# Adding a residual to an open PSUM sum by an accumulating transpose instead of an identity matmul

## The chip, the core and the metric

The kernel runs on one core of a Trainium2 chip. The metric is the device time in microseconds (us). The engines are TensorE (PE; its weight loads are shown as PEld), VectorE (DVE), ScalarE (ACT), GpSimd (POOL) and SyncE (SP).

## The reference

The program chains four small attention layers over 32 sequences of 128 tokens with 128 features. The change touches only the first layer, which has 16 heads of 64 and three layer norms, each over a sum of a projection and a residual:

```
residual = input
sa = _mha(input, input, input, ..., causal=True)
x = _layer_norm(sa + residual, ln1_g, ln1_b)
residual = x
ca = _mha(x, encoder_output, encoder_output, ...)
x = _layer_norm(ca + residual, ln2_g, ln2_b)
residual = x
h = relu(x @ ffn_w1 + ffn_b1)
x = _layer_norm(h @ ffn_w2 + ffn_b2 + residual, ln3_g, ln3_b)
```

Layer 1 is another softmax attention (16 heads of 8), layer 2 consists of three linear-attention blocks with norms, and layer 3 is a softmax attention (8 heads of 16) followed by a recurrence over the 128 tokens.

## The kernel before

The 32 sequences are worked in 8 groups of G = 4 sequences, so a group has 512 token columns. Everything is float32 except the masks. Two streams share the engines: the *main* stream computes the first layer of group g, while the *side* stream computes layers 1 to 3 (up to the recurrence's inputs) of group g-1. `interleave` weaves the steps of the two streams by a fixed table of paces into one written-out order for each engine. So there are 8 main passes, 7 of them with a side stream beside them; then one side pass runs alone, and then come the recurrence (lines 935 and 939) and the output.

Each engine runs its own list strictly in order and waits on semaphores. For PSUM, main uses banks 0 to 4 and side uses banks 5 to 7. A bank is filled by PE (`filled`) and freed by the DVE or ACT instruction that reads it (`emptied`).

A layer norm of the main stream goes like this. POOL keeps `main_residual`, the residual plus the projection's bias, with the features on the partitions and 512 token columns (line 553). PE's item `(tag, "y")`, written by `sums` (lines 648 to 655), fills bank 0 with tokens on the partitions: for each of the 4 sequences it writes a 128x128 block as one accumulation group. For ln1 and ln2 the group is 8 matmuls of `headsT` with `w_o` and one matmul of `main_residual` with the identity. For ln3 it is 4 matmuls of `hidden` (the first four chunks of `headsT`) with `w_f2` and the same identity matmul. As `main_residual` is the stationary operand and the identity the moving one, the identity matmul adds its transpose, token by token. DVE then takes the moments (`bn_stats`, line 1145), POOL raises to the power -1/2, DVE normalises (line 1158), and PE transposes the result back (`turn4`, line 642).

`nc.tensor.transpose` is used elsewhere in the kernel for float32 blocks of the same size: for the probabilities (line 700), for the normalised rows and for `tok` (line 642). In all of these each write starts its own group. The names in the trace read moving operand, stationary operand: `ps<-ident,probs` is a transpose of `probs`, `ps<-ident,main_residual` the identity matmul of this change, and `ps<-w_o_ca,headsT` a projection.

Of the kernel before, what the change touches and what calls it, by code (L numbers as in the profile page):

```python
# [35 lines left out]
C0 = H0 * D0 // 128  # L36
# [3 lines left out]
FC0 = 4  # L40
# [79 lines left out]
def main_fills():  # L120

    order, n = [], 0
    for item in (x for step in MAIN_STEPS for x in step if x[1] not in NO_FILL):
        tag, kind = item[:2]
        if kind == "s":
            bank = item[2] % 2
        elif kind == "o":
            bank = 3
        elif kind == "y":
            bank = 0  # L130
        elif item[:3] == ("ca", "v", 1) and item[3] < 2:
            bank = (1, 3)[item[3]]
        else:
            bank, n = (2, 4)[n % 2], n + 1
        if kind in ("v", "y", "n"):
            by = "D"
        elif kind in ("k", "o") or tag in ("ffn", "in"):
            by = "AD"[item[-1] % 2]
        else:
            by = "A"  # L140
        order.append((item, bank, by))
    return order


def side_fills():

    order = []

    def attention(tag):
        per = SMALL[tag][0]  # L150
        for u in range(per * G + 2):
            if u >= 2 and (u - 1) % per == 0:
                order.append(((tag, "o", (u - 2) // per), 7, "D"))
            if 1 <= u <= per * G:
                order.append(((tag, "t", u - 1), 6, "AD"[u % 2]))
            if u < per * G:
                order.append(((tag, "s", u), 5, "A"))

    order += [(("l1", "q"), 5, "D"), (("l1", "k"), 6, "A"), (("l1", "v"), 7, "D")]
    attention("l1")  # L160
    for blk in ("en", "d0", "d1"):
        order += [((blk, "q"), 5, "D"), ((blk, "k"), 6, "D"), ((blk, "v"), 7, "A"),
                  ((blk, "kv", 0), 5, "D"), ((blk, "kv", 1), 6, "D"),
                  ((blk, "o", 0), 7, "D"), ((blk, "o", 1), 5, "D"), ((blk, "ot"), 6, "A"),
                  ((blk, "y"), 7, "D"), ((blk, "n"), 5, "D")]
        if blk != "d0":
            order += [((blk, "f", 0), 6, "A"), ((blk, "f", 1), 7, "A"),
                      ((blk + "f", "y"), 5, "D"), ((blk + "f", "n"), 6, "D")]
    order += [(("b3", "y"), 5, "D"), (("x3", "y"), 7, "D"), (("b3", "n"), 6, "D"), (("x3", "n"), 5, "D"),
              (("l3", "q"), 6, "D"), (("l3", "k"), 7, "A"), (("l3", "v"), 5, "A")]  # L170
    attention("l3")
    order += [(("l3", "ot"), 5, "A"), (("l3", "x"), 6, "D"), (("z3", "y"), 7, "D"), (("z3", "n"), 5, "D"),
              (("l3", "z"), 6, "A"), (("l3", "u"), 7, "D")]
    return order


MAIN, SIDE = Stream(main_fills()), Stream(side_fills())
# [69 lines left out]
def build_program(nc, I, out):  # L247
    with ExitStack() as ctx:
        def sb(name, shape, dt=F32):
            return ctx.enter_context(nc.sbuf_tensor(name, shape, dt))  # L250
# [7 lines left out]
        ident = sb("ident", [128, 128])  # L258
# [10 lines left out]
        w_o = {t: sb(f"w_o_{t}", [128, C0, E]) for t in ("sa", "ca")}  # L269
        bv_all = {t: sb(f"bv_all_{t}", [128, H0 * D0]) for t in ("sa", "ca")}  # L270
        w_f1 = sb("w_f1", [128, FC0 * 128])
        w_f2 = sb("w_f2", [128, FC0, E])
# [19 lines left out]
        main_residual = sb("main_residual", [128, GT])  # L292
# [3 lines left out]
        headsT = sb("headsT", [128, C0, GT])  # L296
        hidden = headsT[:, 0:FC0, :]
# [40 lines left out]
        residual = neg_q  # L338
# [56 lines left out]
        def bank(st, name):  # L395
            return ps[:, st.bank[name], :]
# [236 lines left out]
        def _(pe):  # L633
            mm = nc.tensor.matmul
# [4 lines left out]
            def turn4(st, name, src):  # L639

                for b in range(G):
                    last = nc.tensor.transpose(bank(st, name)[:, b * 128:b * 128 + 128], src(b), ident[:, :])  # L642
                last.then_inc(filled[st], 1)

            def one(st, name, lhs, rhs):
                mm(bank(st, name)[0:lhs.shape[-1], :], lhs, rhs, start=True, stop=True).then_inc(filled[st], 1)  # L646

            def sums(st, tag, terms):

                for b in range(G):  # L650
                    dst = bank(st, (tag, "y"))[:, b * 128:b * 128 + 128]
                    todo = list(terms(b))
                    for n, (l, r) in enumerate(todo):
                        last = mm(dst, l, r, start=(n == 0), stop=(n == len(todo) - 1))  # L654
                last.then_inc(filled[st], 1)

            def norm_turn(i, st, tag, slot):
# [3 lines left out]
            def token(x, b):  # L661
                return x[:, b * T:b * T + T]

            def before_filling(i, item, *needed):

                held = [MAIN.before[item]] if MAIN.before[item] is not None else []
                wait_all_emptied(pe, i, MAIN, held + list(needed))

            def project(i, item):
                tag, kind, n = item[:3]  # L670
                x = {"sa": xT["a"], "ca": xT["b"] if kind == "q" else cT}[tag]
                if item == ("ca", "v", 0, 0):
                    pe.wait_ge(loaded_ca, n_ca[0])

                needed = {("sa", "k", 0): [("in", 0), ("in", 1)], ("ca", "q", 0): [("ln1", "n")]}
                before_filling(i, item, *needed.get(item, []))
                if kind == "v":
                    one(MAIN, item, token(x, item[3]), w_qkv[tag][:, 2, n * 512:n * 512 + 512])
                else:
                    one(MAIN, item, w_qkv[tag][:, "qk".index(kind), n * 128:n * 128 + 128], x[:, :])  # L680
# [36 lines left out]
            def main(i):  # L717
                for step in MAIN_STEPS:
                    for item in step:
                        tag, kind = item[:2]  # L720
                        if tag == "in":

                            if kind == 0:
                                pe.wait_ge(group_in, i.at(48, 48))
                            turn4(MAIN, item, lambda b: (c_in if kind else x_in)[:, b, :])
                        elif tag == "ffn":
                            before_filling(i, item, ("ln2", "n"))
                            one(MAIN, item, w_f1[:, kind * 128:kind * 128 + 128], xT["a"][:, :])
                        elif kind in ("q", "k", "v"):
                            if item == ("sa", "v", 0, 0):  # L730

                                pe.wait_ge(masks_taken, i.at(1, 1))
                            project(i, item)
                        elif kind == "s":
                            scores(i, item)
                        elif kind == "t":
                            turn(i, item)
                        elif kind == "o":
                            outputs(i, item)
                        elif kind == "y":  # L740
                            pe.wait_ge(main_residual_ready, i.at(3, MAIN_LN.index(tag) + 1))
                            if tag == "ln3":
                                before_filling(i, item, *[("ffn", c) for c in range(FC0)])
                                sums(MAIN, tag, lambda b: [(token(hidden[:, c, :], b), w_f2[:, c, :]) for c in range(FC0)]
                                     + [(token(main_residual, b), ident[:, :])])
                            else:
                                t = "sa" if tag == "ln1" else "ca"
                                before_filling(i, item, *[(t, "o", u) for u in range(UNITS)])
                                sums(MAIN, tag, lambda b: [(token(headsT[:, c, :], b), w_o[t][:, c, :]) for c in range(C0)]
                                     + [(token(main_residual, b), ident[:, :])])  # L750
                        elif kind == "n":
                            before_filling(i, item, (tag, "y"))
                            turn4(MAIN, item, lambda b: main_normed[:, b, :])
                            if tag == "ln3":
                                wait_emptied(pe, i, MAIN, item)
                    yield
# [148 lines left out]
            def setup_side():  # L905
# [19 lines left out]
                yield  # L925

            passes(pe, main, side, setup_side())


# [20 lines left out]
            with pe.Fori(0, GROUPS // 2) as g:  # L950
                for n in range(2):
                    mm(ps[:, n, :], w_c[:, :], ub[:, bass.ds(g * 2 * G + n * G, G), :], start=True, stop=True).then_inc(fin_mm, 1)
                for n in range(2):
                    pe.wait_ge(fin_add, g * 2 + (n + 1))
                    for b in range(G):
                        last = nc.tensor.transpose(ps[:, 2 + n, b * 128:b * 128 + 128],
                                                   fin_sum[n][:, b * T:b * T + T], ident[:, :])
# [476 lines left out]
```

## Time and profile before

| | |
|---|---|
| median of 3 runs | 2710.94 us (2707.78 to 2711.83) |
| profiled execution | 2722.7 us, its span 2721.0 us |
| PE busy | 2321.0 us (85% of the span), 11161 instructions |
| DVE / ACT / POOL busy | 1502.9 / 1168.8 / 340.7 us |
| mean granted TensorE clock | 0.903 of full speed |

The profile page describes one profiled execution. A PE row counts machine instructions: a matmul of the program can be more than one of them, and every MATMUL has its LDWEIGHTS on the PEld row. The ends of matmuls are modelled and overlap with the next ones, so what a matmul costs is read from the distance of the starts and not from its duration. The profiled execution is 11.8 us longer than the median of the timed runs.

### The profile page before, as it was taken

The numbers are of one execution on the slowest core, as the hardware profiler recorded it, in microseconds if no ns is written. First come the engines' busy times: TensorE is split into PE (matmuls) and PEld (weight loads), VectorE is DVE, ScalarE is ACT, GpSimd is POOL, SyncE is SP. The second block draws the span as 40 slices with busy tenths as digits, with TensorE's granted clock in tenths as the row PEclk, the third lists the DMA queues.
The fourth block names the chain that finished last, engine by engine and source line by source line (L and its number), as shares of the span: only waits on it lengthen the run. The fifth ranks groups of instructions, "written<-read, shape, count | busy, mean of one in ns | idle before, by whom it ended". The sixth has DMA issues, their size and how long they took to land.

```text
span 2721.0 us, 32500 instructions
## 1 busy us (share of the span) xinstructions
PE 2321.0 (85%) x11161; PEld 1613.0 (59%) x11161; DVE 1502.9 (55%) x3998; ACT 1168.8 (43%) x4001; POOL 340.7 (13%) x349
## 2 busy tenths in 40 slices
PE   5887988898888988898889888998889888865898
PEld 3555655666565665565556656566556555543596
DVE  4554666565756666566656674666656665233212
ACT  3452635364544645363536454454536353210221
POOL 0002011101112011201110111101120121012000
PEclk9988999999999999999999998999999999566555
DMA  5000000000000000000000000000000000000001
GB/s 152 1 1 13 1 1 1 13 2 1 1 1 13 1 1 1 13 1 1 1 13 1 1 1 1 13 1 1 1 5 1 1 1 1 0 0 0 1 0 31
DMA packets 24511, 19.75 MB, mean 7 GB/s; under 512 B 1699, under 2 KB 22182, under 8 KB 24358
## 3 DMA queue, kind: packets, MB, share of 16 engines
q1 hardware_dynamic: 24358, 17.78, 2.3%
q8 instruction: 87, 1.43, 0.2%
q14 instruction: 66, 0.54, 0.1%
HBM read 15.68 MB, written 2.10 MB: 7 GB/s over the span
## 4 chain that ended last, share of the span: by engine, by line
PE 65%; DVE 21%; ACT 7%; issue 4%; POOL 3%; SPq 0%; DMA 0%; POOLq 0%; DVEq 0%
PE ps L646 13%; PE ps L654 8%; PE ps L787 7%; PE ps L689 7%; PE ps L712 6%; PE ps L770 4%; PE ps L780 4%; DVE tok L1158 3%; PE ps L700 3%; ACT probs L977 3%; DVE keys L1225 2%; PE ps L939 2%; PE ps L642 2%; DVE stats L1145 2%; POOL kx L563 2%
## 5 line engine op out<-in xcount | busy, mean ns | idle before, releaser
L977 ACT ACTIVATE probs<-ps,neg_max 128x128 f32<-128x128 f32 x1024 | 361.8, 366 | 419.4 <-DVE neg_max L1138 412.6
L977 ACT ACTIVATE s_probs<-ps,s_max 128x128 f32<-128x128 f32 x768 | 218.8, 367 | 274.0 <-DVE s_max L1138 273.9
L689 PE MATMUL ps<-keys,queries 128*128 128x256 f32 x1024 | 281.3, 398 | 28.4 <-ACT queries L971 28.4
L712 PE MATMUL ps<-probsT,values 128*128 128x256 f32 x1024 | 277.8, 395 | 3.7 <-ACT headsT L1011 2.7
L787 PE MATMUL ps<-kx,qT 32*128 32x512 f32 (+1 forms) x384 | 244.5, 720 | 33.5 <-POOL kx L563 33.5
L1138 DVE TENSOR_REDUCE neg_max<-ps 128x4 f32<-128x512 f32 x256 | 176.4, 689 | 162.7 <-PE ps L692 161.4
L1138 DVE TENSOR_REDUCE s_max<-ps 128x4 f32<-128x512 f32 x192 | 132.5, 690 | 235.7 <-PE ps L787 233.5
L689 PEld LDWEIGHTS ps<-keys,queries 128*128 128x128 f32 x1024 | 187.4, 195 | 119.6 <-ACT queries L971 42.4
L540 POOL TENSOR_TENSOR rstd<-var_eps,minus_half 128x4 f32<-128x4 f32 x88 | 90.3, 1026 | 1235.3 <-DVE var_eps L1151 1234.6
L1145 DVE BATCH_NORM_STATS2 stats<-ps 128x6 f32<-128x128 f32 x352 | 78.2, 284 | 299.4 <-PE ps L654 295.6
L712 PEld LDWEIGHTS ps<-probsT,values 128*128 128x128 f32 x1024 | 178.8, 194 | 67.3 <-issue 25.1
L977 ACT ACTIVATION_READ_ACCUMULATOR probs<-ps,neg_max 128x1 f32 x1024 | 208.7, 204 | 0.0
L700 PEld LDWEIGHTS ps<-ident,probs 128*128 128x128 f32 x1024 | 123.5, 142 | 128.2 <-issue 81.9
L971 ACT ACTIVATE probsT<-ps 128x512 f32<-128x512 f32 x256 | 155.7, 608 | 50.7 <-PE ps L700 49.5
L770 PEld LDWEIGHTS ps<-l1v,s_probsT 128*128 128x128 f32 x1024 | 143.9, 209 | 51.9 <-issue 49.3
L700 PE MATMUL ps<-ident,probs 128*128 128x128 f32 x1024 | 158.6, 278 | 0.4 <-DVE probs L1181 0.4
L642 PE MATMUL ps<-ident,tok 128*128 128x128 f32 x352 | 61.6, 302 | 103.8 <-DVE tok L1158 89.6
L646 PE MATMUL ps<-xT_a,w_qkv_sa 128*128 128x512 f32 x256 | 132.1, 603 | 12.8 <-DVE cT L1210 11.0
L780 PE MATMUL ps<-ident,s_probs 128*128 128x128 f32 x768 | 133.0, 300 | 10.3 <-ACT s_probs L977 7.3
L534 POOL TENSOR_TENSOR pool_scratch<-minus_half 128x1 f32<-128x1 f32 x88 | 17.0, 193 | 985.0 <-DVE x1T L1275 672.1
L770 PE MATMUL ps<-l1v,s_probsT 128*128 128x9 f32 x1024 | 137.1, 261 | 0.7 <-ACT s_probsT L971 0.7
L1240 DVE COPY headsT<-ps 64x256 f32<-64x256 f32 x256 | 107.5, 420 | 40.3 <-PE ps L712 38.2
(211 smaller groups left out, 4088.9 us busy)
## 6 DMA issues: line engine op xcount, KB each, us to landing
x_in<-in_x SPq DMA_DIRECT2D x8, 256.0 KB, 3.0
c_in<-in_ctx SPq DMA_DIRECT2D x8, 256.0 KB, 3.3
skip_in<-in_mask_BxS_ik SPq DMA_DIRECT2D x8, 256.0 KB, 3.1
out<-x_all SPq DMA_DIRECT2D x8, 256.0 KB, 2.3
valid_in<-in_mask_BxS_bf SPq DMA_DIRECT2D x8, 64.0 KB, 3.4
w_qkv_sa<-in_L_xattn_sa_wq SPq DMA_DIRECT2D x1, 512.0 KB
w_qkv_sa<-in_L_xattn_sa_wk SPq DMA_DIRECT2D x1, 512.0 KB
w_qkv_sa<-in_L_xattn_sa_wv SPq DMA_DIRECT2D x1, 512.0 KB
```

Source lines behind the costliest of these rows:

```text
L646: mm(bank(st, name)[0:lhs.shape[-1], :], lhs, rhs, start=True, stop=True).then_inc(filled[st], 1)
L654: last = mm(dst, l, r, start=(n == 0), stop=(n == len(todo) - 1))
L689: mm(bank(MAIN, item)[:, n * 256:n * 256 + 256], queries[:, c % 2, at], keys[:, c % 2, :, at], start=(n == 0), stop=False, skip_group_chec ...
L700: last = nc.tensor.transpose(bank(MAIN, item)[:, h * 128:h * 128 + 128], probs[:, u % 3, h * 128:h * 128 + 128], ident[:, :])
L712: last = mm(bank(MAIN, item)[:, n * 256:n * 256 + 256], values[:, c // 4, b0 + n, (c % 4) * 128:(c % 4) * 128 + 128], probsT[:, u % 2, n * ...
L770: last = mm(bank(SIDE, (tag, "o", b))[:, at:at + d1], s_probsT[:, u % 2, h * 128:h * 128 + 128], value[:, b, q * 4 + h, :], start=True, st ...
L780: last = nc.tensor.transpose(bank(SIDE, (tag, "t", u))[:, h * 128:h * 128 + 128], s_probs[:, u % 2, h * 128:h * 128 + 128], ident[:, :])
L787: mm(bank(SIDE, (tag, "s", s)), qT[part, b * T:b * T + T], kx[part, :, b * T:b * T + T], start=True, stop=True).then_inc(filled[SIDE], 1)
L971: A(dst, view(s) if view else s, fn, **kw).then_inc(emptied[st, "A"], 1)
L977: last = A(dst[:, u % dst.shape[1], h * 128:h * 128 + 128], bank(st, (tag, "s", u))[:, h * 128:h * 128 + 128], ACT.Exp, bias=src_max[:, u ...
L1138: V.tensor_reduce(dst[:, u % 2, :], bank(st, (tag, "s", u)).rearrange("p (h k) -> p h k", h=4), AX.X, ALU.max, negate=True).then_inc(max_r ...
L1145: last = V.bn_stats(stats[:, slot, b, :], bank(st, (tag, "y"))[:, b * 128:b * 128 + 128])
```

## The change

`sums` gets an argument `residual`. With it, the accumulation group is left open after the last projection matmul, and the group is closed by a matmul with `is_transpose=True` and `start=False` on the same operands as before. The three calls of the main stream's norms use it. The calls of the side stream pass no residual and are as they were. Nothing is reordered, no wait or semaphore is added or removed, and the program has the same list of instructions on each engine.

```
-            def sums(st, tag, terms):
+            def sums(st, tag, terms, residual=None):

                 for b in range(G):
                     dst = bank(st, (tag, "y"))[:, b * 128:b * 128 + 128]
                     todo = list(terms(b))
                     for n, (l, r) in enumerate(todo):
-                        last = mm(dst, l, r, start=(n == 0), stop=(n == len(todo) - 1))
+                        last = mm(dst, l, r, start=(n == 0), stop=(residual is None and n == len(todo) - 1))
+                    if residual is not None:
+                        last = mm(dst, token(residual, b), ident[:, :], start=False, stop=True, is_transpose=True)
                 last.then_inc(filled[st], 1)
...
-                                sums(MAIN, tag, lambda b: [(token(hidden[:, c, :], b), w_f2[:, c, :]) for c in range(FC0)]
-                                     + [(token(main_residual, b), ident[:, :])])
+                                sums(MAIN, tag, lambda b: [(token(hidden[:, c, :], b), w_f2[:, c, :]) for c in range(FC0)],
+                                     main_residual)
...
-                                sums(MAIN, tag, lambda b: [(token(headsT[:, c, :], b), w_o[t][:, c, :]) for c in range(C0)]
-                                     + [(token(main_residual, b), ident[:, :])])
+                                sums(MAIN, tag, lambda b: [(token(headsT[:, c, :], b), w_o[t][:, c, :]) for c in range(C0)],
+                                     main_residual)
```

## Rows read from the trace of the kernel before

**Rows 1.** The page: span, busy times, the slices of PE and its clock, the chain.

```profile
span 2721.0 us, 32500 instructions
PE 2321.0 (85%) x11161; PEld 1613.0 (59%) x11161; DVE 1502.9 (55%) x3998; ACT 1168.8 (43%) x4001; POOL 340.7 (13%) x349
...
PEclk9988999999999999999999998999999999566555
...
PE 65%; DVE 21%; ACT 7%; issue 4%; POOL 3%; SPq 0%; DMA 0%; POOLq 0%; DVEq 0%
```

**Rows 2.** Lines 654 and 700: count, duration ns min/median/max, first and last start.

```profile
L654 PEld LDWEIGHTS ps<-ident,main_residual x192: 192/192/212, 106.1 to 2299.3; 128*128 128x128 f32 x192
L654 PE MATMUL ps<-ident,main_residual x192: 275/275/276, 106.2 to 2299.4; 128*128 128x128 f32 x192
...
L700 PE MATMUL ps<-ident,probs x1024: 272/273/421, 40.4 to 2270.5; 128*128 128x128 f32 x171
```

**Rows 3.** Timeline, 499.9 to 512.5 us: start, length, engine, line [idle before, releaser].

```profile
499.81 0.96 PE L770 MATMUL ps<-l3v,s_probsT 128*128 128x17 f32 x8
...
503.00 2.02 PE L654 MATMUL ps<-w_o_ca,headsT 128*128 128x128 f32 x16 [1.04 <-DVE headsT L1240]
...
505.08 1.95 PE L654 MATMUL ps<-w_o_ca,headsT 128*128 128x128 f32 x16
...
507.09 1.95 PE L654 MATMUL ps<-w_o_ca,headsT 128*128 128x128 f32 x16
...
510.89 0.39 PE L654 MATMUL ps<-ident,main_residual 128*128 128x128 f32 x2
...
511.11 0.60 PE L642 MATMUL ps<-ident,tok 128*128 128x128 f32 x4
511.31 0.89 DVE L1145 BATCH_NORM_STATS2 stats<-ps 128x6 f32<-128x128 f32 x4 [8.46 <-PE ps L654]
511.75 0.60 ACT L971 ACTIVATE kx<-ps 128x512 f32<-128x512 f32 x1 [10.98 <-PE ps L642]
```

**Rows 4.** Timeline of PE, 420 to 432 us: transposes, then a matmul.

```profile
425.41 0.60 PE L700 MATMUL ps<-ident,probs 128*128 128x128 f32 x4
425.85 1.03 PE L712 MATMUL ps<-probsT,values 128*128 128x256 f32 x4
```

**Rows 5.** The chain that ended last, in order of time: start, length, what.

```profile
104.35 8.28 PE ps L654 x72
...
228.51 4.72 PE ps L654 x40
...
369.46 8.29 PE ps L654 x72
...
1253.79 8.29 PE ps L654 x72
...
1546.37 8.29 PE ps L654 x72
...
1844.15 8.29 PE ps L654 x72
...
2274.69 8.28 PE ps L654 x72
...
2294.99 4.72 PE ps L654 x40
```

**Rows 6.** Three ln2 sums by windows: PE, PEld, DVE, ACT, POOL busy, granted clock, DMA.

```profile
205.79:215.61 9.82, 9.80 (x72) 9.62 (x72) 0.00 (x0) 0.00 (x0) 0.00 (x0) 0.84 0.01 2
...
503.00:511.28 8.28, 8.28 (x74) 8.28 (x75) 0.00 (x0) 0.00 (x0) 0.00 (x0) 1.00 0.01 2
1680.15:1690.04 9.89, 9.88 (x74) 9.89 (x75) 0.00 (x0) 0.00 (x0) 0.00 (x0) 0.83 0.00 0
```

**Rows 7.** Timeline of PE, 204 to 218 us: the head of the first of them.

```profile
205.79 3.55 PE L654 MATMUL ps<-w_o_ca,headsT 128*128 128x128 f32 x16 [1.49 <-DVE l_bo L1128]
```

**Rows 8.** Groups by line and shape: count, busy us, mean ns of one, idle before.

```profile
L770 PE MATMUL ps<-l3v,s_probsT 128*128 128x17 f32 x512 | 69.0, 268 | 0.7 <-ACT s_probsT L971 0.7
```

## The prediction

> **What bounds the kernel now.** I read the page first. PE is busy for 85% of the span and holds 65% of the chain that ended last; DVE has 21%, ACT 7% and POOL 3% [rows 1]. So time taken off PE counts wherever PE is what the others wait for. The question is whether it is in the sums that are changed.
>
> Second comes the chain in order of time [rows 5]. Each sum of a main norm is a piece of its own in it: a piece of 72 PE instructions for ln1 and ln2, a piece of 40 for ln3. I counted 16 pieces of the first kind (first at 104.35 us, last at 2274.69 us) and 8 of the second (first at 228.51, last at 2294.99): 2 and 1 for each of the 8 passes. All 24 sums are therefore on the chain, in their full length (8.28 and 4.72 us).
>
> Third is the timeline around one sum [rows 3]. The sum starts at 503.00 and the DVE instruction that reads it starts at 511.31, having been idle for 8.46 us, released by PE's line 654. ACT had been idle for 10.98 us when it got the transpose that PE does right behind the sum. During the sum DVE and ACT do nothing at all: their busy times in that window are zero, and POOL's too [rows 6]. So no other work stands beside a sum that could become the later one when the sum gets shorter, and PE's own list behind the sum moves up with it.
>
> **What is removed.** The program has 8 passes x 3 norms x 4 sequences = 96 identity matmuls of `main_residual`. The trace has 192 MATMUL and 192 LDWEIGHTS for them [rows 2]: a float32 matmul is two machine instructions of each kind. The duration (275 ns) is not the price, since they overlap. The price is the distance of starts: from 505.08 to 507.09, 2.01 us, PE starts 18 instructions (16 of the projection and 2 of the residual) [rows 3], which is 0.1117 us each. All 192 ran at this speed: their durations lie between 275 and 276 ns [rows 2]. Removed: 192 x 0.1117 = 21.4 us.
>
> **What is added.** 96 float32 transposes of 128x128. The same form stands in the trace at line 700: the 8 passes have 8 x 32 units of 4 transposes, 1024 in all, and the trace has 1024 MATMUL for them [rows 2]: one machine instruction each, not two. Four of them start at 425.41, and the next matmul at 425.85 [rows 4]: 0.44 / 4 = 0.110 us each. Added: 96 x 0.110 = 10.6 us.
>
> The sum is 10.6 - 21.4 = **-10.9 us** (before rounding), 0.113 us for each residual and 0.45 us for each of the 24 sums. A sum of 72 instructions becomes one of 68 and should last 7.83 in place of 8.28 us; one of 40 becomes 36, 4.27 in place of 4.72 us.
>
> **Changing over between the two kinds.** The changed group goes matmul, transpose, matmul, and the kernel before has both crossings. From matmul to transpose: the last two residual instructions start at 510.89 and the transposes of `tok` at 511.11 [rows 3], 0.22 us for two instructions, the usual distance. From transpose to matmul: the 0.110 us above holds the crossing from line 700 to line 712 already [rows 4]. So the crossing is worth nothing. What the trace does not show is a transpose that adds to a block that the matmul just ahead is still writing. I bound its slot. From below: matmuls that move only 17 columns start every (0.96 - 0.268) / 7 = 0.10 us [rows 3, 8], so a full 128x128 float32 load does not let two starts come closer. That would be 96 x 0.10 = 9.6, and -11.8 us. From above: the transpose runs without overlap for its whole 0.273 us [rows 2], 96 x 0.273 = 26.2, which is +4.8 us. I take 0.110, the row of the same operation. Plain matmuls add to the block of their predecessor at the full rate already in these very sums, and that is the reason to stay at this end.
>
> **What comes behind.** Nothing is reordered and no wait is new. `filled` is raised by the last transpose in place of the last matmul, and the modelled length of both is alike (273 against 275 ns) [rows 2]. DVE's moments, POOL's root and the rest come 0.45 us earlier after every sum. POOL's `main_residual` is made before the sum as it was, and PE's wait for it was never the last one (the trace names DVE for it [rows 3]).
>
> **The clock.** Two of the 16 long sums took 9.82 and 9.89 us, at a granted clock of 0.84 and 0.83, where the usual one takes 8.28 at 1.00 [rows 6]. The delay is in the head: the first 16 matmuls take 3.55 in place of 2.02 us [rows 3, 7], after PE had been idle for the DVE (1.49 us). These are two levels, 2.4 GHz and 1.2 GHz, mixed in one stretch. The clock also makes equal passes unequal: from ln1's sum to the next pass's it is 292.6 us (1253.79 to 1546.37) and then 297.8 us (1546.37 to 1844.15), with a mean of (1844.15 - 369.46) / 5 = 294.9 us [rows 5]. Passes that get 1.36 us shorter meet the clock's changes at other places, and the total can move by some microseconds either way from that alone. The three timed runs differ by 4 us, which is my measure of it.
>
> The Trainium skill (TensorE: Matmul & The Clock Gate, Part 4: PE-mode transpose) says that the full clock does not engage for transposes since they do not count as PE being busy in the same way. By that rule a sum with 4 transposes among 32 matmuls would keep the full clock less surely. The rows of this kernel speak against its mattering: the four transposes at 425.41 started every 0.11 us, the full rate. The same page's terms table calls the transpose mode 4 times faster for float32, which applied to the removed 0.223 us would be 0.056 us for a transpose and -16.1 us in all; the 0.110 us of line 700 doesn't agree.
>
> **The rivals.**
> - *The transpose is cheaper between matmuls.* At line 700 transposes follow each other with a load each, so 0.110 us could be the load's pace. If a lone one took half a slot, the gain is 96 x (0.2234 - 0.056) = 16.1 us: 2694.8. Against it: the load of 128x128 float32 is needed here too, and matmuls of 17 columns are no closer than 0.10 us. Chance 5%.
> - *Half is given back.* Something other than the sum would have to end the waits behind it, or the clock would take it back, say in the passes that are now well placed (292.6 us): 2705.5. For it: the spread of the passes. Against it: every sum is on the chain, with DVE and ACT idle. Chance 8%.
> - *The clock falls in more sums.* The price is 9.82 - 8.28 = 1.54 us for each, so 7 more of the 24 eat the gain, and 12 more give 18.5 - 10.9 = +7.6: 2718.5. Against it: only 4 of 36 starts are transposes. Chance 4%.
> - *The accumulating transpose drains the array (the slower side).* Place: the end of each of the 96 groups. If the transpose waits until the matmul ahead has written and the next group waits for the transpose, each costs 0.273 + (0.275 - 0.112) = 0.436 us, 41.9 us in all against 21.4 removed, +20.5: 2731. With the first wait alone it is +4.8: 2716. It decides from a slot of 0.223 us on. Against it: both crossings show nothing. Chance 4%.
> - *The change does not do what it says*, that is, the accumulating form still becomes two instructions with two loads: 0, 2711. Line 700's one instruction speaks against it. Chance 3%.
>
> **How the numbers follow.** The forecast has 76%. Against the profiled execution it is 2722.7 - 10.9 = 2711.8 us; that execution lies 11.8 us above the median of the runs, and no step of mine depends on why, so the timed result is 2710.94 - 10.9 = **2700.1**, given as 2700. The likeliest case's own range is 2695 to 2706 (the bounds -11.8 and the clock's few microseconds). The range for 8 in 10 takes in the cheaper transpose in part and the half given back: 2693 to 2708. A measurement of this kernel can tell about 0.2%, 5.4 us, from no change. Faster by more than that: nearly all of the forecast, half of the second rival and the first one, 79%. Within it: the rest of these, the change that does nothing and the drain with one wait, 14%. Slower: most of the clock rival and the full drain, 7%.
>
> **What would show it.** In the changed profile the residual's row has 96 MATMUL and not 192, PE has 11161 - 96 = 11065 instructions, up to missing records, the pieces of the chain read x68 at about 7.83 us and x36 at about 4.27 us, and DVE's idle time before the moments shrinks by 0.45 us each. I am wrong if a group's starts show a gap beside the transpose, if more sums run with a granted clock under 1.00, or if the sums are shorter and the passes are not.

## The result: slower by 0.3%, with the work saved as forecast

| | before | after |
|---|---|---|
| median | 2709.7 us (9 runs, 2707.78 to 2714.22) | 2718.54 us (9 runs, 2716.18 to 2722.37) |
| profiled execution | 2722.7 us, span 2721.0 | 2716.18 us, span 2714.4 |
| ratio after / before | | 1.0031 (95% interval 1.0023 to 1.0040) |

The forecast was 2700 us (2693 to 2708), so it was wrong in sign. Later the changed kernel ran again beside before in two other groups of runs (e5 and e12 below). It took 2718.92 and 2719.00 us there, with ratios of 1.0030 (1.0019 to 1.0041) and 1.0006 (0.9995 to 1.0017). So its own time repeats to 0.5 us, and what varies is before, whose median lay between 2709.7 and 2717.24 us from group to group. The 0.3% holds in two of the three comparisons; in the third no difference is shown. The page of the profile after, against [rows 1]:

```profile
span 2714.4 us, 32308 instructions
PE 2314.5 (85%) x11065; PEld 1598.9 (59%) x11065; DVE 1503.5 (55%) x3998; ACT 1168.9 (43%) x4001; POOL 340.3 (13%) x349
...
PEclk9998999899999999999989999999989999566555
...
PE 65%; DVE 21%; ACT 7%; issue 4%; POOL 3%; SPq 0%; DMA 0%; POOLq 0%; DVEq 0%
```

PE starts 11065 instructions, 96 fewer, as forecast. The residual's own rows, against [rows 2], from the view of line 656:

```profile
L656 PEld LDWEIGHTS ps<-ident,main_residual x96: 142/143/175, 106.9 to 2295.2; 128*128 128x128 f32 x96
L656 PE MATMUL ps<-ident,main_residual x96: 272/273/273, 107.0 to 2295.3; 128*128 128x128 f32 x96
```

One sum in the timeline after (start, length, engine, line), against [rows 3]:

```profile
798.20 1.95 PE L654 MATMUL ps<-w_o_ca,headsT 128*128 128x128 f32 x16
799.98 0.27 PE L656 MATMUL ps<-ident,main_residual 128*128 128x128 f32 x1
800.09 1.95 PE L654 MATMUL ps<-w_o_ca,headsT 128*128 128x128 f32 x16
...
803.77 0.27 PE L656 MATMUL ps<-ident,main_residual 128*128 128x128 f32 x1
...
804.09 0.89 DVE L1147 BATCH_NORM_STATS2 stats<-ps 128x6 f32<-128x128 f32 x4 [8.00 <-PE ps L656]
```

A sequence takes 800.09 - 798.20 = 1.89 us where it took 2.01, there is no gap on either side of the transpose, and DVE is idle for 8.00 us before the moments where it was 8.46. So the sum is 0.46 us shorter at full clock (forecast: 0.45). The local forecast holds; the total does not follow it.

### The profile page after: what moved, and what is told of

Read it like the earlier page. It is cut to its first block, busy times and chain, and to the rows that moved or that the text cites. A ratio compares the mean times of both kernels' runs of the same rounds, so it can differ in the third digit from the quotient of the medians.

```text
span 2714.4 us, 32308 instructions
## 1 busy us (share of the span) xinstructions
PE 2314.5 (85%) x11065; PEld 1598.9 (59%) x11065; DVE 1503.5 (55%) x3998; ACT 1168.9 (43%) x4001; POOL 340.3 (13%) x349
## 4 chain that ended last, share of the span: by engine, by line
PE 65%; DVE 21%; ACT 7%; issue 4%; POOL 3%; SPq 0%; DMA 0%; POOLq 0%; DVEq 0%
PE ps L646 14%; PE ps L654 8%; PE ps L789 7%; PE ps L691 7%; PE ps L714 6%; PE ps L772 4%; PE ps L782 4%; PE ps L702 3%; DVE tok L1160 3%; ACT probs L979 3%; DVE keys L1227 2%; PE ps L941 2%; PE ps L642 2%; DVE stats L1147 2%; POOL kx L563 2%
```

## Where the time went: the clock, pass by pass

The first profile of before was of an execution 11.8 us above the median of its three runs, and in span the changed kernel is even shorter than that one. For a comparison I need an execution of before that is like its timed runs. Run e1 (below) gave one: 2710.55 us, span 2708.8 us, the fastest of its twelve. Here are its passes, cut at the start of the transposes of `x_in`. The columns are: the stretch, its length, the busy times of PE, PEld, DVE, ACT and POOL, the granted clock, DMA.

```profile
18.20:237.30 219.10, 173.61 (x803) 117.25 (x803) 109.78 (x264) 98.18 (x356) 8.34 (x9) 0.95 0.12 34
237.30:532.30 295.00, 259.13 (x1317) 178.10 (x1317) 182.53 (x480) 142.86 (x484) 41.96 (x41) 0.97 0.01 4
532.30:829.40 297.10, 261.35 (x1316) 179.26 (x1316) 182.49 (x480) 142.86 (x484) 41.96 (x41) 0.96 0.01 4
829.40:1123.00 293.60, 257.29 (x1317) 177.28 (x1317) 182.87 (x480) 142.87 (x484) 42.19 (x41) 0.98 0.01 4
1123.00:1416.50 293.50, 257.23 (x1316) 177.17 (x1316) 182.79 (x480) 142.87 (x484) 42.20 (x41) 0.98 0.01 4
1416.50:1710.00 293.50, 257.26 (x1316) 177.24 (x1316) 182.80 (x479) 142.86 (x484) 42.19 (x41) 0.98 0.01 4
1710.00:2003.60 293.60, 257.26 (x1317) 177.24 (x1317) 182.84 (x480) 142.86 (x484) 42.19 (x41) 0.98 0.01 4
2003.60:2560.70 557.10, 445.80 (x1908) 293.97 (x1908) 262.88 (x712) 191.53 (x614) 75.95 (x73) 0.79 0.00 1
```

The same view of the changed kernel:

```profile
18.10:235.50 217.40, 171.96 (x792) 115.51 (x791) 109.82 (x265) 98.11 (x356) 8.33 (x9) 0.95 0.12 34
235.50:532.60 297.10, 261.24 (x1305) 178.90 (x1305) 182.49 (x480) 142.57 (x484) 41.91 (x41) 0.96 0.01 4
532.60:827.10 294.50, 257.79 (x1305) 176.14 (x1305) 182.90 (x480) 142.59 (x484) 42.13 (x41) 0.97 0.01 4
827.10:1120.80 293.70, 257.43 (x1305) 176.38 (x1305) 182.60 (x480) 142.58 (x484) 41.88 (x41) 0.97 0.01 4
1120.80:1415.80 295.00, 258.67 (x1305) 177.08 (x1305) 182.56 (x480) 142.58 (x484) 41.90 (x41) 0.96 0.01 4
1415.80:1711.40 295.60, 259.59 (x1304) 177.26 (x1304) 182.57 (x480) 142.58 (x484) 41.90 (x41) 0.96 0.01 4
1711.40:2006.30 294.90, 258.62 (x1304) 177.02 (x1304) 182.56 (x480) 142.56 (x484) 41.89 (x41) 0.96 0.01 4
2006.30:2566.30 560.00, 448.98 (x1896) 294.44 (x1897) 262.75 (x712) 191.16 (x614) 75.60 (x73) 0.78 0.00 1
```

I number the passes from 0, so the first row is pass 0 and the last row is pass 7 with the side pass behind it. In this execution, before settles from the fourth row on into passes of 293.5 us with a clock of 0.98, each like the last to 0.1 us. The changed kernel does not: its passes take 293.7 to 297.1 us at 0.96 to 0.97. DVE, ACT and POOL have the same busy times in all. The first pass is 1.7 us shorter after, the six with a full side stream are 4.5 us longer together where 6 x 1.36 = 8.2 us less was due, and the last row is 2.9 us longer.

The clock's share: the engine spends twice the missing clock at the low level (1.2 GHz), so e1 has 2 x (1 - 0.907) x 2708.8 = 504 us of it and the changed kernel 2 x (1 - 0.900) x 2714.4 = 543 us. These 39 us more cost 5.6 + 10.9 = 16.5 us, or 0.42 us each, if the forecast saving is all there. Before's own runs give this price without that assumption: e1's slowest run has 2 x (1 - 0.902) x 2724.7 = 534 us of low time and is 15.9 us longer than the fastest with 504 us, which is about 0.5 us for each us more. So the low time is enough to eat the saving, and there is no sign that the saving is missing.

A second look is where both kernels meet the same low stretches. Before's pass of 297.1 us has them at about -1 (double length), 122, 142, 224 (double) and 279 us after its start. So has the changed kernel's of 295.6 us, all within 1 us of these. The difference is 1.5 us; forecast for a pass were 1.36. Alone this would be weak: e10's passes of 296.9 us have the same five stretches too, and are only 0.2 us shorter than before's where 0.67 was due. The firmest sign of the saving stays the sum itself, 0.46 us shorter in the timeline above.

## The experiments

Theory A: only the shorter sums matter; they put the work elsewhere against the clock's changes, and the passes then meet more low stretches. Rival B: the transposes themselves keep the clock up less well. Four kernels at a time ran on one chip and shared the runs of before. The three groups had before at 2717.24 us (e1 to e4), 2711.54 (e5 to e8) and 2715.92 (e9 to e12).

**e1: before again.** No edit.

> The kernel before, unchanged, to get a second trace of it with the granted clock of every run. Theory A (the saving of 10.9 us on PE is real, and the changed kernel's clock is low for longer because its work lies elsewhere against the clock's changes): about 2710 us, ratio 1.000, with a mean clock above the 0.898 of the changed kernel's runs, by so much that the low time explains some 20 us. Rival B (transposes keep the clock up less well than matmuls): the same for this run.

2715.86 us, ratio 1.0001 (0.9987 to 1.0015). Its 12 runs go from 2710.55 us at a clock of 0.907 to 2726.46 us at 0.902, a wider spread than I had allowed for. The changed kernel's nine lie at 0.897 to 0.900: at a lower clock than any run of before for which the clock is on record, and still faster than before's slowest.

**e2: half of the residuals.** The start count of the changed kernel without a transpose.

```
                     todo = list(terms(b))
+                    if st is MAIN and b not in (0, 2):
+                        todo = todo[:-1]
```

> The kernel before without the identity matmul in sequences 1 and 3 of each group of 4, so the residual is left out for half of the sequences. It starts exactly as many PE instructions fewer as the changed kernel (4 in each of the 24 sums, 0.45 us), and has no transpose in a sum. Theory A (only the shorter sums and where they put the work against the clock): like the changed kernel, about 2718 us. Rival B (transposes count less for the clock): 2710 - 10.7 = 2699 us, the saving comes out in full.

2715.34 us, ratio 0.9993 (0.9982 to 1.0004), clock 0.898 to 0.900. Of the saving of 10.7 us about 2 us are left in the medians, with no transpose in a sum.

**e3: transposes with the old length.** The edit is to the changed kernel.

```
+                    if residual is not None:
+                        nc.tensor.transpose(dst, token(residual, b), ident[:, :])
                     for n, (l, r) in enumerate(todo):
```

> The changed kernel with one more transpose of main_residual ahead of each group (the group's first matmul overwrites it), so that each sum has the length of the kernel before, with 8 transposes in it. Theory A: the time of the kernel before, about 2710 us. Rival B: more transposes and so more low clock, at least the 2718 us of the changed kernel and up to 2718 + 20.

2728.67 us, ratio 1.0042 (1.0028 to 1.0056). My number for A missed and B's came in. The trace shows how: passes 1 and 2 are 294.7 and 297.1 us, as before's; then where before goes over to 293.5, this one stays at 296.9 to 297.0 us for the four that are left. The padded sum is not quite as long as before's: from its first start to the next item's it lasts 8.05 us (796.05 to 804.10) against 8.11 (503.00 to 511.11 [rows 3]), and the ln3 sum is shorter by as much, so a pass has about 0.2 us less work. Whether that or the transposes hold it back, e3 can't tell. e9 does.

**e4: no residuals.** `b not in ()` in e2's edit.

> The kernel before with no identity matmul in any sum of the main stream, so the residual is left out. Each of the 24 sums is 0.89 us shorter, 21.4 us in all. Rival B: 2710 - 21.4 = 2688.6 us. Theory A: not in line with the saving; the 21.4 us less what the clock takes or gives, anywhere from 2680 to 2710 us, since the work lies elsewhere once more.

2706.7 us, ratio 0.9959 (0.9945 to 0.9972): 11 us faster where the work is 21.4 us less, clock 0.902 in the profiled run. Again some 10 us are lost, and there is no transpose in a sum.

**e5: after again.** No edit.

> The changed kernel, unchanged, on this chip beside the padded ones. Theory A (each pass is 1.36 us shorter at equal clock, and what decides the total is how often the passes meet the clock's low stretches): its passes alternate between about 294.9 and 295.6 us again, so 2716 to 2719 us and the same against the kernel before within 0.4%. Rival B (transposes in a sum lower the clock): clearly slower than the kernel with half of the residuals left out, which has the same count of instructions.

2718.92 us, ratio 1.0030 (1.0019 to 1.0041). The passes alternate between 295.6 and 294.9 us from the third to the sixth, as expected.

**e6: padded plus one.** e3 with this in front of the transposes of `x_in`, k = 1:

```
+                            if kind == 0:
+                                for _ in range(k):
+                                    nc.tensor.transpose(bank(MAIN, item)[:, 0:128], x_in[:, 0, :], ident[:, :])
                             turn4(MAIN, item, lambda b: (c_in if kind else x_in)[:, b, :])
```

> The padded kernel (e3), with one more transpose at the start of each of the 8 main passes, overwritten by the next: 8 x 0.11 = 0.9 us more work. Theory A: the passes of e3 stay at 297.0 us with 7 low pieces each because each begins just short of the place from which the kernel before goes over to 293.5 us; 0.11 us more carries pass 3 or 4 past it, and the kernel gets faster by up to 5 x 3.5 = 17 us, about 2712 us, although it does more. Rival B: slower than e3 by 1 us, about 2729 us.

2727.58 us, ratio 1.0059 (1.0045 to 1.0073): a miss for A as I had put it. The passes did not leave the long pattern; they took 296.9 to 297.0 us as in e3. But the run could not test A. The added transpose falls into a wait: the next matmuls on PE's list read `x_side`, and PE waits there for VectorE. In e3 they start at 1125.40, 1.12 us after the pass (1124.28), and in e6 at 1132.23, 1.13 us after it (1131.10). So nothing behind the transpose came later, and the equal passes say nothing about the clock. The same holds for e7, where the rows stand.

**e7: before plus one.** The same edit on before, k = 1.

> The kernel before with one more transpose at the start of each main pass: 0.9 us more work. Theory A: passes of 293.6 us from the third on, and since they begin 0.1 us later against the clock's grid each time rather than 0.02 us earlier, they do not fall back as some runs of the kernel before do: 2709 to 2713 us, not slower than before and less scattered. Rival B, or any theory by work alone: 0.9 us slower than before, about 2718 us.

2720.87 us, ratio 1.0040 (1.0026 to 1.0053), from 5 runs. Here is the start of pass 5, first in e1 and then in e7 (start, length, engine, line, idle time before):

```profile
1416.50 0.66 PE L642 MATMUL ps<-ident,x_in 128*128 128x128 f32 x4 [1.55 <-DVE xT_b L1171]
1417.63 1.16 PE L646 MATMUL ps<-x_side,turned 128*128 128x512 f32 x2 [0.47 <-DVE qT L1258]
...
1417.11 0.33 PE L727 MATMUL ps<-ident,x_in 128*128 128x128 f32 x1 [1.55 <-DVE xT_b L1174]
...
1418.24 1.13 PE L646 MATMUL ps<-x_side,turned 128*128 128x512 f32 x2 [0.36 <-DVE qT L1261]
```

The matmuls of `x_side` start 1.13 us after the pass in both; PE's wait for VectorE is 0.11 us shorter and takes in the added transpose. The profiled execution (span 2712.6 us, the fastest of the five) has the passes that A named: 297.1 us in pass 2, then 293.6, 293.5, 293.6, 293.5. As the added work is hidden, that is no support for A. The timed runs missed A's 2709 to 2713 us: four of the five have a clock of 0.902 or 0.903, where 12 of the 17 runs of before in the same group have 0.907 or 0.908. So an instruction that fits into a wait of PE went with a kernel 9 us slower in the median, at a lower clock.

**e8: after plus three.** The same edit on after, k = 3.

> The changed kernel with three more transposes at the start of each main pass: 0.33 us each pass, 2.6 us of work in all. By work alone: 2.6 us slower than e5. Theory A: the alternation of 294.9 and 295.6 us cannot hold, the passes take another pattern, and the time differs from e5 by something other than 2.6 us, of either sign and up to 10 us.

Three transposes no longer fit into the wait: the matmuls of `x_side` start 1.55 us after the pass (823.98 to 825.53) and not 1.13. The time is 2715.47 us, ratio 1.0010 (0.9998 to 1.0022), against e5's 2718.92 and 1.0030 (1.0019 to 1.0041): 3.4 us less, with 2.6 us more work. The intervals touch, so that it is faster is likely and not certain; that it is 2.6 us slower is excluded. Passes 3 and 4 are 295.6 and 294.9 us as in e5; the last two (1414.50 to 2003.60) are not: 292.9, then 296.2 us.

**e9: one residual less in a pass.**

```
+                    if tag == "ln3" and b == 3:
+                        todo = todo[:-1]
```

> The kernel before without one identity matmul in each pass (ln3, the last sequence of each group, whose residual is left out): 2 PE starts less in each pass, 0.22 us, 1.8 us in all, and no transpose in any sum. Theory A (pass length against the clock's grid): a pass that meets the long pattern is now about 0.2 us too short to leave it, as with the padded kernel, and stays at 297.0 us with low pieces at -1, 122, 142, 224 and 279 us: slower than before by 5 to 12 us although it does less work. By work alone, and by rival B: 1.8 us faster than before.

2730.65 us, ratio 1.0051 (1.0034 to 1.0068). This is the clearest of the runs: one matmul taken out of each pass, nothing else, and the kernel is some 14 us slower (A had said 5 to 12, work alone 1.8 us faster). The profiled execution is the fastest of its six runs (2722.59 us). Its passes 2 to 5:

```profile
527.90:821.80 293.90, 258.09 (x1315) 177.49 (x1315) 182.50 (x480) 142.57 (x484) 41.90 (x41) 0.97 0.01 4
821.80:1118.60 296.80, 261.09 (x1314) 178.97 (x1314) 182.40 (x480) 142.59 (x484) 41.90 (x41) 0.96 0.01 4
1118.60:1415.60 297.00, 261.24 (x1315) 179.11 (x1315) 182.51 (x480) 142.58 (x484) 41.89 (x41) 0.96 0.01 4
1415.60:1712.50 296.90, 261.18 (x1314) 179.05 (x1314) 182.40 (x479) 142.59 (x484) 41.88 (x41) 0.96 0.01 4
```

It is the pattern of e3 without a transpose. The two have nearly the same work in a pass, 0.22 and about 0.2 us less than before's; e3 has 8 transposes in every sum and e9 none. So the long passes don't come from the transposes. To see where in the pass the clock is low, three windows of 10 us, at -3, 117 and 137 us from the start of pass 5; first e1:

```profile
1413.50:1423.50 10.00, 6.26 (x24) 4.07 (x24) 8.87 (x18) 1.29 (x2) 5.62 (x6) 0.83 0.10 27
1533.50:1543.50 10.00, 7.69 (x41) 5.25 (x39) 5.65 (x16) 2.93 (x6) 2.77 (x3) 1.00 0.00 0
1553.50:1563.50 10.00, 7.16 (x32) 3.72 (x30) 7.65 (x22) 1.86 (x3) 2.75 (x3) 1.00 0.00 0
```

then e9:

```profile
1412.60:1422.60 10.00, 7.31 (x24) 4.41 (x24) 7.95 (x18) 1.28 (x2) 5.21 (x6) 0.66 0.07 27
1532.60:1542.60 10.00, 7.69 (x29) 4.64 (x28) 5.55 (x18) 2.65 (x5) 2.77 (x3) 0.83 0.00 0
1552.60:1562.60 10.00, 7.98 (x40) 5.32 (x39) 5.43 (x18) 0.00 (x0) 2.74 (x3) 0.83 0.00 0
```

The second and third window are at full clock in e1 and have a low stretch in e9, and the first has more of one. PE is busy for 7.2 to 8.0 of 10 us in the second and third in both: the same stretch of program keeps the clock in one kernel and loses it in the other. The second window in the timeline of PE, first e1, then e9:

```profile
1536.42 0.66 PE L642 MATMUL ps<-ident,tok 128*128 128x128 f32 x4 [2.31 <-DVE tok L1158]
...
1538.21 1.88 PE L646 MATMUL ps<-encT,w_l2f_en 128*128 128x512 f32 x4
...
1536.08 0.66 PE L642 MATMUL ps<-ident,tok 128*128 128x128 f32 x4 [2.31 <-DVE tok L1160]
...
1538.33 3.11 PE L646 MATMUL ps<-encT,w_l2f_en 128*128 128x512 f32 x4
```

PE has waited 2.31 us for VectorE in both. Behind the wait the same four matmul instructions take 1.88 us in e1 and 3.11 us in e9. Before the stretch at 142 us there is such a wait too, 2.01 us in e1 (at 1556.43) and 2.02 us in e9 (at 1557.79).

**e10: three of four.** `b not in (0, 1, 2)` in e2's edit.

> The kernel before without the identity matmul in the last sequence of every main sum (its residual is left out): 2 PE starts less in each of the 24 sums, 0.67 us a pass, 5.4 us in all, no transposes. By work alone and by rival B: 5.4 us faster than before. Theory A: not 5.4 us faster but anywhere from 10 us slower to 10 us faster, with mean granted clock lower than before's wherever it is not faster.

2711.91 us, ratio 0.9983 (0.9972 to 0.9995): 4.6 us faster where the work is 5.4 us less. In the median this is what the work alone says, so the time decides nothing, and it shows that a shorter pass need not lose. Its profiled passes do jump, between 293.5 and 296.9 us:

```profile
825.30:1118.80 293.50, 257.71 (x1310) 176.90 (x1310) 182.42 (x479) 142.86 (x484) 41.98 (x41) 0.97 0.01 4
1118.80:1415.70 296.90, 260.95 (x1310) 178.53 (x1310) 182.54 (x480) 142.88 (x484) 41.97 (x41) 0.96 0.01 4
```

These are nearly the two lengths of e1's and e9's passes, though this kernel has 0.67 us less work in each than before. The pass of 293.5 us runs at 0.97 here and at 0.98 in e1: more low time takes the place of the work that was saved.

**e11 and e12: half of the residuals and after, side by side.** The edit of e2, and none.

> The kernel of e2 again, now on the same chip and in the same rounds as the changed kernel, with the same count of PE starts as that. Theory A: the same alternation of passes and the same time as e12 within 3 us. Rival B: faster than e12 by up to 10 us, with a clearly higher clock.

> The changed kernel a third time, beside e11: 2717 to 2720 us with a mean clock of 0.898 by either theory. What counts is its distance from e11: within 3 us by theory A, up to 10 us by rival B.

e11: 2716.15 us, ratio 1.0000 (0.9990 to 1.0009). e12: 2719.00 us, ratio 1.0006 (0.9995 to 1.0017). They are 2.85 us apart. From the second pass on the two have the same passes, first e11:

```profile
529.90:827.60 297.70, 261.46 (x1305) 178.24 (x1305) 182.48 (x480) 142.59 (x484) 41.90 (x41) 0.95 0.01 4
827.60:1123.20 295.60, 259.63 (x1305) 177.30 (x1305) 182.49 (x480) 142.60 (x484) 41.89 (x41) 0.96 0.01 4
1123.20:1418.10 294.90, 258.64 (x1305) 177.06 (x1305) 182.45 (x480) 142.59 (x484) 41.90 (x41) 0.96 0.01 4
...
2008.60:2568.60 560.00, 449.06 (x1897) 294.51 (x1897) 262.53 (x712) 191.18 (x614) 75.60 (x73) 0.78 0.00 1
```

then e12:

```profile
531.70:829.30 297.60, 261.39 (x1304) 178.19 (x1304) 182.45 (x479) 142.59 (x484) 41.89 (x41) 0.95 0.01 4
829.30:1124.90 295.60, 259.60 (x1304) 177.30 (x1304) 182.53 (x479) 142.60 (x484) 41.90 (x41) 0.96 0.01 4
1124.90:1419.80 294.90, 258.61 (x1304) 177.03 (x1304) 182.46 (x479) 142.58 (x484) 41.88 (x41) 0.96 0.01 4
...
2010.30:2570.30 560.00, 449.05 (x1897) 294.49 (x1897) 262.56 (x712) 191.16 (x614) 75.60 (x73) 0.78 0.00 1
```

Length, clock and busy times agree to 0.1 us and 0.01. One has a transpose for every residual; the other has no transpose in a sum, and the same number of PE starts. Rival B falls with that, and with e3 and e9 above; the 2.85 us are the most that it could still claim.

## Why the prediction was wrong

- **What is removed and added: right.** 96 starts fewer; a sequence 0.12 us (0.11 was forecast) and a sum 0.46 us shorter; no crossing cost, no drain. The rival with the cheaper transpose is out: 1.89 us are 17 starts at 0.111, so the transpose has one full slot and not half of one.
- **All 24 sums on the chain, nothing takes their place: right** as far as the traces show. DVE still waits for every sum (8.00 us in the one above), and with the same low stretches a pass is 1.5 us shorter.
- **"Two of the 16 long sums" and "the total can move by some microseconds either way": the step that failed.** I looked for the clock's effect in the sums, took it for scatter around zero, and put nothing for it into the sum. It lies elsewhere in the pass (about 122 and 142 us after its start, one ahead of ln1's sum and one behind it), and it was not zero in the mean: at the low level the changed kernel spends 39 us more than e1, which ate the 10.9 us and 5.6 us on top. The three timed runs, 4 us apart, were too few to size it: before's runs go from 2706.59 to 2726.46 us without any change of the program. Before has a good pattern, 293.5 us a pass with a clock of 0.98, and a small change can lose it: e7 was 9 us slower than its group's before though the added work is hidden, and e9 was 14 us slower with 0.22 us of work less in a pass. It isn't a law: e10 kept most of its saving.
- **How good before's pattern was depended on the group.** In the group of e5 to e8, 12 of before's 17 runs have a clock of 0.907 or 0.908. In the other two groups, e1 included, it is 3 of 70, and before's medians (2717.24 and 2715.92 us) are 4 to 8 us above the other two (2711.54 and 2709.7 us). The clocks of the result's own nine runs of before are not on record; their times (2707.78 to 2714.22 us) are those of the good pattern. Why the groups differ is open.
- **"No step of mine depends on why" the profiled execution was 11.8 us above the median: wrong as well.** That was the clue. Cut like e1's, that trace has two passes in the good pattern (831.5 to 1418.5) and then leaves it; its last row is 6.8 us longer than e1's 557.1 with the same work. The 292.6 and 297.8 us that I read in [rows 5] are cut at ln1's sum and lie around that exit. I averaged them to 294.9 us and thereby took as usual what was an excursion. The rows are the last good pass, the first one behind it, and the last row:

```profile
1125.00:1418.50 293.50, 257.29 (x1316) 177.25 (x1316) 182.74 (x479) 142.59 (x484) 42.13 (x41) 0.98 0.01 4
1418.50:1714.20 295.70, 258.76 (x1316) 178.50 (x1316) 182.65 (x479) 142.59 (x484) 42.12 (x41) 0.97 0.01 4
...
2009.00:2572.90 563.90, 453.82 (x1909) 299.87 (x1909) 262.44 (x712) 191.27 (x614) 75.59 (x73) 0.78 0.00 1
```

- **The rivals.** "Half is given back" named the right mechanism ("the passes that are now well placed") at half the saving: against this result's before 18 to 20 us were lost, against e12's 14 us, and not 5. "The clock falls in more sums" gave 2718.5 us, the measured number, by luck: it needed 12 more slow sums, and the changed kernel's trace has two of its 16 long sums at a low clock (202.6 us at 0.84, 499.2 us at 0.82), as many as before's. The Trainium skill (TensorE: Matmul & The Clock Gate, Part 4: PE-mode transpose) says that the full clock does not engage for transposes. That pointed to the right sign, but it isn't the reason here: e11 and e12 have the same clock.

What stays open: what exactly decides whether the stretches at 122 and 142 us are granted the full clock; why some executions of before leave the short pattern and others don't, and more of them in one group than in another; and the last 2.85 us between e11 and e12, of which the profiled executions show only that they differ before the second pass. That the passes settle where they do because the clock's changes don't move with the program is my reading of e3, e9 and e10, and it is not shown: no run could move the clock's changes themselves, and e7's timed runs are slower although its passes got no more work on their path. None of the edited kernels that compute the whole reference (the changed one, e3, e6, e7 and e8) is faster than before.

## What to carry to other kernels

In a program that repeats a stage and leaves PE partly idle, compare the stage's length and granted clock repetition by repetition before trusting a saving of some tenths of a per cent. Repetitions with the same work that differ by 3.5 us, as here, show that the clock decides more than the saving. Then a small change of the stage, even one that takes work out or one that fits into a wait, can cost more than it saves. A local saving is then best judged in the timeline of the changed instructions, and the total by many runs of both kernels in several groups, since before's own median moved by 7.5 us here.

## What the runs showed of the hardware

- An accumulating float32 transpose of 128x128 into an open group costs one PE start (0.11 us) and the identity matmul two (0.223 us), with no gap on either side (after, e12).
- Passes of this kernel come in few lengths: 293.5 us (e1), 297.0 us (e3 and e9, with about 0.2 us less work in a pass), both to 0.2 us in e10 (0.67 us less work), or 294.9 and 295.6 us in turn (e5, e11 and e12, 1.34 to 1.36 us less).
- Behind the same wait of 2.31 us for VectorE, four float32 matmul instructions of 512 columns took 1.88 us in one kernel and 3.11 us in another that differs by one matmul in a pass.
- Time at the low clock costs this kernel about 0.5 us for each us of it (e1's fastest and slowest run).
- Taking one float32 matmul out of each pass of 295 us made the kernel slower by 0.51% (0.34 to 0.68%), and adding a transpose that fits into a wait of PE by 0.40% (0.26 to 0.53%).
